# FFN weights of a transformer kernel turned by DMA transfers instead of TensorE, with POOL, ACT and DVE queues reordered

## The reference, cut to what matters

```python
def block_qdq_weight(w, block=32, bits=4):       # w_gate, w_up: (1376, 512), w_down: (512, 1376)
    wb = w.reshape(out_f, in_f // block, block)
    scale = jnp.maximum(jnp.max(jnp.abs(wb), axis=-1, keepdims=True) / 7, 1e-12)
    wq = jnp.clip(jnp.round(wb / scale), -8, 7) * scale
xq = act_qdq(x)                                  # 16 bits, one scale for the whole tensor
up = act_qdq(xq @ wu.T)
gate = act_qdq(xq @ wg.T)
sig = fixed_qdq(jax.nn.sigmoid(gate), 1 / 65536)
gate = act_qdq(gate * sig)
o = act_qdq(gate * up)
return o @ wd.T
```

## Time and profile before

| | |
|---|---|
| median of 3 runs | 828.37 us (827.33 to 829.54) |
| the profiled execution, time | 830.54 us |
| its span, first to last instruction | 828.5 us |
| TensorE busy | 728.5 us (88%) |
| DVE busy | 643.6 us (78%) |
| ACT busy | 513.9 us (62%) |
| POOL busy | 511.3 us (62%) |
| mean granted TensorE clock | 0.954 |

### The profile page before, as it was taken

One profiled execution on the slowest core, in us unless ns is written; L12 is line 12 of the kernel. 1 busy time (PEld: TensorE's weight loads), 2 busy tenths in 40 slices (PEclk: granted clock), 3 DMA queues, 4 the chain that ended last, 5 costly groups with the idle time before them and its releaser, 6 DMA issues.

```text
span 828.5 us, 13514 instructions
## 1 busy us (share of the span) xinstructions
PE 728.5 (88%) x3443; PEld 342.7 (41%) x3443; DVE 643.6 (78%) x1374; ACT 513.9 (62%) x968; POOL 511.3 (62%) x488
## 2 busy tenths in 40 slices
PE   0688999736695996999999999999999788999998
PEld 0234545313232452444444444444444253444443
DVE  6885667678799678888888888888888767656655
ACT  4656766556857436777777777777776643655540
POOL 1986675546566557778888888888884414344330
PEclk9999999976888898999999999999999999999998
DMA  7211232201225326788666666666655512332311
GB/s 320 89 65 39 65 101 67 62 26 51 39 51 95 121 70 133 178 191 180 124 146 144 144 144 145 142 146 144 152 102 102 102 39 80 107 110 84 114 38 51
DMA packets 164500, 89.08 MB, mean 108 GB/s; under 512 B 154081, under 2 KB 154337, under 8 KB 161522
## 3 DMA queue, kind: packets, MB, share of 16 engines
q1 hardware_dynamic: 164466, 88.67, 42.9%
HBM read 49.85 MB, written 1.05 MB: 61 GB/s over the span
## 4 chain that ended last, share of the span: by engine, by line
PE 60%; DVE 13%; POOL 12%; issue 9%; DMA 2%; ACT 2%; SPq 1%; DVEq 0%; POOLq 0%; ACTq 0%
PE ps L950 19%; PE ps L951 19%; PE ps L952 19%; POOL arena L464 4%; POOL arena L472 3%; DVE arena L1290 3%; DVE arena L1293 2%; PE ps L1138 1%; POOL arena L604 1%; DMA arena<-arena 1%; DVE arena L1287 1%; POOL arena L451 1%; ACT arena L647 1%; POOL arena L482 1%; DVE ss L1449 1%
## 5 line engine op out<-in xcount | busy, mean ns | idle before, releaser
L950 PE MATMUL ps<-arena 128*128 128x512 f16 (+2 forms) x996 | 385.9, 388 | 25.7 <-DVE arena L1293 11.8
L951 PE MATMUL ps<-arena 128*128 128x512 f16 (+2 forms) x996 | 384.6, 386 | 0.0
L952 PE MATMUL ps<-arena 128*128 128x512 f16 (+2 forms) x996 | 384.2, 386 | 0.0
L647 ACT ACTIVATE arena<-arena 128x512 f16<-128x512 f32 (+9 forms) x392 | 260.8, 692 | 98.1 <-POOL arena L604 29.6
L1293 DVE SCALAR_TENSOR_TENSOR arena<-ps,arena 128x512 f32<-128x512 f32 (+2 forms) x182 | 122.9, 702 | 53.4 <-ACT arena L647 45.9
L950 PEld LDWEIGHTS ps<-arena 128*128 128x128 f16 (+1 forms) x996 | 99.5, 100 | 148.2 <-issue 34.6
L952 PEld LDWEIGHTS ps<-arena 128*128 128x128 f16 (+1 forms) x996 | 99.5, 100 | 122.6 <-issue 11.3
L951 PEld LDWEIGHTS ps<-arena 128*128 128x128 f16 (+1 forms) x996 | 99.5, 100 | 111.7 <-issue 9.2
L604 POOL TENSOR_SCALAR arena<-arena,rden 128x512 f32<-128x512 f32 x128 | 114.9, 898 | 25.3 <-DVE rden L1639 16.1
L1287 DVE TENSOR_TENSOR arena<-arena 128x512 f16<-128x512 f32 (+2 forms) x146 | 108.7, 779 | 5.3 <-ACT arena L647 4.8
L846 ACT ACTIVATE arena<-arena,mneg 128x512 f32<-128x512 f32 x124 | 88.5, 715 | 36.8 <-DVE mneg L1619 36.8
(11 more groups left out here) (126 smaller groups left out, 702.4 us busy)
## 6 DMA issues: line engine op xcount, KB each, us to landing
arena<-in_moe_w SPq DMA_DIRECT2D x18, 768.0 KB, 4.4
arena<-in_ffn_w SPq DMA_DIRECT2D x33, 256.0 KB, 2.7
arena<-in_wq SPq DMA_DIRECT2D x8, 1024.0 KB, 5.3
arena<-in_wo SPq DMA_DIRECT2D x8, 1024.0 KB, 5.3
arena<-in_kv_w SPq DMA_DIRECT2D x4, 1024.0 KB, 5.1
arena<-arena SPq DMA_TRANSPOSE x144, 3.3
arena<-in_ctx SPq DMA_DIRECT2D x1, 2048.0 KB, 9.5
arena<-in_ctx_t SPq DMA_DIRECT2D x1, 2048.0 KB, 13.9
```

What stands on the lines that cost most here:

```text
L647: return a.activation(out_, in_, ACT.Copy, scale=scale, bias=bias)
L950: pe.matmul(out_, lhs[0], rhs[0], start=first, stop=False)
L951: pe.matmul(out_, lhs[0], rhs[1], start=False, stop=False)
L952: return pe.matmul(out_, lhs[1], rhs[0], start=False, stop=last)
```

## The change

- A chunk isn't transposed by TensorE. `scale_back` writes `deq[n % 4]` (DQ = 4 buffers), ACT's `weight_high` copies it (from SBUF) to the first half of `wt[n % 4]`, the low half goes to the second half, and SP turns both with one DMA transposition of 128 x 1024 f16 into `wfx[n % 11]` (`turn_w`). `tile` waits for the landing.
- The low halves of even chunks from 14 on are POOL's (`low`), the others DVE's.
- Scales and their inverses are made for two chunks at once (`pair_scales`); the factor SW = 64 goes into the scales and into the first rounding copy.
- Five raw buffers instead of four; the load of chunk n+6 stands behind the turn of chunk n in SP's list. `turn_k` stands behind all turns of chunks and behind a wait for their landing.
- Turn n of each list now holds: ACT `weight_high(n+2)`, `round_weights(n+3)`, `tile_out(n)`; POOL `low(n+2)` (its chunks), `scale_back(n+3)`, `divide(n+4)`; DVE maxima of n+6, low half of n+2 (its chunks), the extrema of tile n-2, on odd n the scales of a pair.
- Value units 8 to 15 use banks 2 and 3 in turn instead of bank 4 alone, and wait for the copy before the last one.
- The split of the key weights moves to gate tiles 15 to 20. `s16` has four buffers: sigmoid i waits for `gated(i-4)` instead of `gated(i-2)`. `k_pow` and `k_low` stand one turn earlier in POOL's list.

```diff
-RAW = 4
+RAW = 5
+DQ = 4
+SB = 4
...
+def low_owner(n):
+    return 0 if n >= FT + 2 and n % 2 == 0 else 1
+def low_count(n):
+    return sum(low_owner(m) == low_owner(n) for m in range(n + 1))
...
-        wf = [carve(104, (WS, D), F16), carve(115, (WS, D), F16)]
+        wfx = carve(104, (WS, 2 * D), F16)
+        wf = [wfx[:, :, 0:D], wfx[:, :, D:2 * D]]
+        wt = carve(56, (DQ, 2 * D), F16)
+        deq = carve(64, (DQ, D))
...
-        s16 = carve(10, (2, TOK), U16)
+        s16 = carve(8, (SB, TOK), U16)
...
-        deq = [carve(202, (D,)), carve(8, (D,))]
...
+        w_lo = [sem("w_lo0"), sem("w_lo1")]
+        w_tr = [sem(f"w_tr{i}") for i in range(DQ)]
...
+            def turn_w(n):
+                sp.wait_ge(w_lo[low_owner(n)], low_count(n))
+                if n >= WS:
+                    sp.wait_ge(f_ps, n - WS + 1)
+                sp.dma_start_transpose(wfx[:, n % WS].rearrange("p (a b) -> p a b", b=P),
+                                       wt[:, n % DQ]).then_inc(w_tr[n % DQ], 16)
...
+            ring(RAW)
...
-            plain_loop(sp, RAW, FT + 5, ring)
-            kw_load(3)
-            plain_loop(sp, FT + 5, NCH, ring)
+            for n in range(2):
+                turn_w(n)
+                ring(n + RAW + 1)
+            for n in range(2, NCH):
+                turn_w(n)
+                if n + RAW + 1 < NCH:
+                    ring(n + RAW + 1)
+                if n == FT + 1:
+                    kw_load(3)
+            for i in range(DQ):
+                sp.wait_ge(w_tr[i], 16 * ((NCH - 1 - i) // DQ + 1))
...
             def divide(n):
-                g.wait_ge(w_inv, n + 1)
+                g.wait_ge(w_inv, n // 2 + 1)
...
-                if n >= 2:
-                    g.wait_ge(w_t, n - 1)
-                g.tensor_tensor(deq[n % 2].rearrange("p (a b) -> p a b", b=QB), v, s, ALU.mult).then_inc(w_deq, 1)
+                if n >= DQ:
+                    g.wait_ge(w_lo[low_owner(n - DQ)], low_count(n - DQ))
+                g.tensor_tensor(deq[:, n % DQ].rearrange("p (a b) -> p a b", b=QB), v, s, ALU.mult).then_inc(w_deq, 1)
+            def low(n):
+                g.wait_ge(w_hi, n + 1)
+                g.tensor_tensor(wt[:, n % DQ, D:2 * D], deq[:, n % DQ], wt[:, n % DQ, 0:D], ALU.subtract)\
+                    .then_inc(w_lo[0], 1)
...
             def weights(n):
-                scale_back(n)
-                if n + 2 < NCH:
-                    divide(n + 2)
+                if n + 2 < NCH and low_owner(n + 2) == 0:
+                    low(n + 2)
+                if n + 3 < NCH:
+                    scale_back(n + 3)
+                if n + 4 < NCH:
+                    divide(n + 4)
...
+            scale_back(0)
...
-            scale_back(0)
-            for u in range(4, MT - 1):
-                v_low(u)
-            g.wait_ge(xt_ps, KD)
...
+            v_low(4)
+            v_low(5)
+            v_low(6)
+            scale_back(2)
...
-            weights(2)
+            weights(0)
...
-                    weights(3 + k)
+                    weights(1 + k)
...
-                weights(2 * j + 4)
+                weights(2 * j + 2)
...
-                weights(2 * j + 5)
+                if j < 4:
+                    weights(2 * j + 3)
...
-                weights(2 * j + 14)
-                weights(2 * j + 15)
+                weights(2 * j + 11)
+                if j == 2:
+                    kw_scale(3, 0)
+                    kw_scale(3, 1)
+                weights(2 * j + 12)
+                if j == 2:
+                    kw_scale(3, 2)
+                    kw_scale(3, 3)
...
-                if k < 3:
-                    weights(20 + k)
-                kw_scale(3, k)
-            weights(2 * FT + 1)
-            weights(2 * FT + 2)
-            for k in range(KD):
+                weights(17 + k)
...
-            for i in range(2, FT - 1):
-                weights(2 * FT + 1 + i)
-                u = i // 2 - 2
-                if i % 2 == 0 and u >= 0:
+            weights(2 * FT - 1)
+            weights(2 * FT)
+            for i in range(1, FT - 1):
+                weights(2 * FT + i)
+                u = i // 2 - 1
+                if i % 2 and u >= 0:
...
-            for u in range(3, 2 * MT):
+            for u in range(4, 2 * MT):
...
-                copy(w, w, 1.0, MAGIC).then_inc(w_mag, 1)
+                copy(w, w, SW, MAGIC).then_inc(w_mag, 1)
...
-                src = bank(2 + u % 2 if u < MT else 4)
+                src = bank(2 + u % 2)
...
+            def weight_high(n):
+                a.wait_ge(w_deq, n + 1)
+                if n >= DQ:
+                    a.wait_ge(w_tr[n % DQ], 16 * (n // DQ))
+                copy(wt[:, n % DQ, 0:D], deq[:, n % DQ]).then_inc(w_hi, 1)
...
-            for u in range(3, MT - 1):
-                v_out(u)
+            v_out(3)
+            v_out(4)
+            weight_high(0)
+            v_out(5)
+            v_out(6)
...
+            weight_high(1)
...
-            def weight_high(n):
-                a.wait_ge(w_t, n + 1)
-                if n >= WS:
-                    a.wait_ge(f_ps, n - WS + 1)
-                copy(wf[0][:, n % WS], bank(2 + n % 2), SW).then_inc(w_hi, 1)
...
             def tile_turn(n, dst):
-                weight_high(n + 1)
+                weight_high(n + 2)
...
-            weight_high(0)
...
-                if n >= 2 * FT - KD:
-                    kw_high(3, [n - 2 * FT + KD])
+                if FT + 6 <= n < FT + 6 + KD:
+                    kw_high(3, [n - FT - 6])
...
-                if i >= 2:
-                    a.wait_ge(gs_done, i - 1)
+                if i >= SB:
+                    a.wait_ge(gs_done, i - SB + 1)
...
-                if i < FT - 1:
-                    weight_high(2 * FT + i + 1)
+                if i < FT - 2:
+                    weight_high(2 * FT + i + 2)
...
-                if u >= MT:
-                    pe.wait_ge(v_cp, u)
-                elif u >= 2:
+                if u >= 2:
...
-                kv_product(c, m, bank(2 + u % 2 if u < MT else 4)).then_inc(v_ps, 1)
+                kv_product(c, m, bank(2 + u % 2)).then_inc(v_ps, 1)
...
-            pe.wait_ge(xt_lo, 1)
...
-            def weight_transposes(n):
-                pe.wait_ge(w_deq, n + 1)
-                if n >= 2:
-                    pe.wait_ge(w_lo, n - 1)
-                for k in range(4):
-                    mm = pe.transpose(bank(2 + n % 2)[:, k * P:(k + 1) * P], deq[n % 2][:, k * P:(k + 1) * P],
-                                      ident[:, :])
-                mm.then_inc(w_t, 1)
...
-                pe.wait_ge(w_lo, n + 1)
+                pe.wait_ge(w_tr[n % DQ], 16 * (n // DQ + 1))
...
-            def step(base, i, odd):
-                weight_transposes(base + i + 1)
-                tile(base, i, odd)
...
-            pe.wait_ge(v_cp, MT)
-            weight_transposes(0)
...
-                step(0, i, i % 2)
+                tile(0, i, i % 2)
...
-                    step(0, i, i % 2)
+                    tile(0, i, i % 2)
...
-                step(FT, i, (FT + i) % 2)
+                tile(FT, i, (FT + i) % 2)
...
-            weight_transposes(2 * FT + 1)
...
-            for u in range(5):
-                weight_transposes(2 * FT + 2 + 2 * u)
+            for u in range(6):
...
-                if u < 4:
-                    weight_transposes(2 * FT + 3 + 2 * u)
-            k_unit(5)
...
-            pe.wait_ge(w_lo, NCH)
+            for i in range(DQ):
+                pe.wait_ge(w_tr[i], 16 * ((NCH - 1 - i) // DQ + 1))
...
-            def scales(n, maxima):
-                own.wait(maxima)
-                s = one(dsc, n % SC)
-                return own.mark(ts(s, s, 1.0 / 7.0, ALU.mult, TINY, ALU.max))
-            def inverse_scales(n, scaled):
-                own.wait(scaled)
-                v.reciprocal(one(dsi, n % SC), one(dsc, n % SC)).then_inc(w_inv, 1)
-            def block_scales(n):
-                inverse_scales(n, scales(n, block_maxima(n)))
+            def pair_scales(n):
+                own.wait(own.n)
+                at = (n - n % 2) % SC
+                both = [flat(w[:, at:at + n % 2 + 1]) if n % 2 else w[:, at] for w in (dsc, dsi)]
+                own.link(ts(both[0], both[0], SW / 7.0, ALU.mult, SW * TINY, ALU.max))
+                v.reciprocal(both[1], both[0]).then_inc(w_inv, 1)
...
-                stt(one(wf[1], n % WS), bank(2 + n % 2), SW, one(wf[0], n % WS), ALU.mult, ALU.subtract).then_inc(w_lo, 1)
+                tt(wt[:, n % DQ, D:2 * D], deq[:, n % DQ], wt[:, n % DQ, 0:D], ALU.subtract).then_inc(w_lo[1], 1)
...
-            for n in range(3):
-                block_scales(n)
+            for n in range(4):
+                block_maxima(n)
+                if n % 2:
+                    pair_scales(n)
...
-                m = block_maxima(n + 3)
-                weight_low(n)
-                m = scales(n + 3, m)
+                if n + 6 < NCH:
```

(60 more changed lines are left out.)

6 lines of the change are left out of this document (3 added, 3 removed).

## The result

The changed kernel takes 826.65 us (median, 824.89 to 828.05), the kernel before 828.24 us (825.86 to 833.61), both on one chip. The ratio is 0.9971, 95% interval 0.9958 to 0.9985: faster by 2.4 us (1.6 us between the two medians), where 10.8 us were forecast. The direction was right, the size was not: 826.65 lies just above the range of 809 to 826, and the gain is one that the forecast itself called hard to tell from none (under 0.3%). The profiled execution has 825.1 us of span against 828.5, with a mean granted clock of 0.943 (0.954 before).

The account below looks back on a forecast made before the run. TensorE bounds up and early gate tiles; a row of work across engines bounds the last gate tiles and sigmoid stage; DVE times-up. -10.5 (to gate's end) - 0.3 (sigmoid) = -10.8: 819.7 profiled, 817.5 us median; own range 813 to 822, wide range 809 to 826.

Parts of the forecast that it names:

- Parameters of up keep their 2.7 us hole: End of up stage: hole unchanged, last value unit ends 110.7, first gate tile 113.5 against 118.4, -4.9 us.
- its last ends +35: Gate tail: DVE's last extrema end 35 us after tile 14, at 161.4 against 171.97; -10.5 us in all.
- not on the path: Pairs of scales: one multiply and reciprocal per two weights save at most 0.5 us of DVE a weight, off the path.
- A set: Transposition set on TensorE: 0.45 us each; 22 of 33 count where TensorE is the bound, 9.9 us at most.
- Pairs: Two tiles with one value unit: new latency hides, so a pair takes 7.75 us instead of 8.64.
- the POOL-ACT loop: Rounding, scale-back and divide take 3.5 us per weight; hidden in pairs, the bound where tiles follow without value units.
- the key turn takes it back: Sigmoid stage: ACT waits for turn_k(0) behind all weight landings, losing the 5.5 us gained; 48.5 us, -0.3 us.
- Rival 1: Sigmoid stage: key turn isn't late, landing before ACT's copy; -10.5 - 6.5, 811 us; chance 0.12.
- rivals 2 and 4: 2: POOL-ACT loop shows, pairs 8.2, 823 us, chance 0.24. 4: no split fits, pairs 9.4, 828 us, chance 0.08.
- Rival 3: Transposition landing too long: gain gone at 5.9 us, at 6.5 us the run takes 834 us; chance 0.08.
- the old price of a late gate tile: Last gate tiles, kernel before: one takes 5.9 us, TensorE waiting for POOL's scale-back, then DVE's low half.
- The low half was priced 0.7: DVE's low half of a weight: 0.7 us, rounded up from four in 2.48.

Follow-up runs that it names:

- the 16 matmuls: Changed kernel plus 16 TensorE matmuls, whose results nothing reads, in the hole ahead of the parameters of up: 825.56 us, ratio 0.9947 to the kernel before.
- the four combined kernels: Changed kernel with key turns earlier and five up conversions later (821.56 us); adding low halves on DVE (822.80), 16 matmuls (821.09), maxima 16 behind up's parameters (820.20).

## Why the prediction was wrong

**The step that failed first** is "Parameters of up keep their 2.7 us hole, since tile_out(10) ends level with the last value unit". The value unit ended 0.7 us later than forecast (111.4 against 110.7), and ACT was no obstacle (tile 10 out at 110.6). But DVE had its own turn 10 and a pair of scales ahead of three extrema groups, and its queue set the moment: first gate tile at 116.12 instead of 113.5. I had walked ACT, POOL and TensorE through this place, and DVE not; in the queue order its extra work could be read. The longer hole then cost the clock level, which the forecast allowed for only ahead of tile 20: 4.7 us for a tile of 2.6. Together the second gate tile came 4.7 us later than forecast: 0.7 from the value unit, 1.9 from the longer hole, 2.1 from the clock. The earlier parameters with DVE's turn moved show the part of the hole, the 16 matmuls that of the clock.

**The second term mis-sized** is the gate tail, "its last ends +35". The walk of POOL's queue was right: from the end of tile 14 (131.4) tile 20 started at +22.5 as forecast, tile 21 went out from +31.0 as forecast, and the lower clock in tile 20, which the forecast had allowed for, was hidden ahead of it. DVE's last work ended at +37.1: extrema and conversions as counted, but a pair of scales stood between, which the forecast had called "not on the path" and which took 1.3 us there, and a conversion took 1.19 us instead of 0.54. So the parameters of gate came at 168.52 and not 161.4: 4.7 up to the second gate tile, 2.1 from the tail and 0.3 between them, -3.5 us where -10.5 stood. That DVE's list sets this end is shown by the five conversions moved away; what the stretching alone costs, no run shows.

**What held.** A set is worth 0.44 us where TensorE is the bound. Pairs take 7.77 us (7.75 forecast), the POOL-ACT loop 3.46 (3.5), the turn lands 3.1 us after its issue (4.9 at most), from the end of low half 20 (150.7) to tile 20 it is 3.1 us where 3.5 were taken with 0.3 for semaphores, tile 0 starts at 69.74 (70.0). In the sigmoid stage the forecast was that sigmoids and loop gain 5.5 and the key turn takes it back, 48.5 us: it took 48.43, 42.98 without the key turn's place in the queue, and 53.14 without the two further buffers. Rival 1's 6.5 us were measured as 5.4. Times-up was unchanged. The times of rivals 2 and 4 (823 and 828) bracket the result, but the mechanism of neither was there: the loop did not show in the pairs. Rival 3 needed landings over 5.9 us; none came, even with a second turn for each weight. The 5.9 us that the forecast read as the old price of a late gate tile is one gap of several: from set to set the kernel before has 3.2, 5.9 and 6.5 us from 151.87 on. The sum does not use it.

**What the sum missed besides.** The low half was priced 0.7 by a row that reads PSUM. The new one reads two operands from SBUF. Groups by shape, DVE, changed kernel, 70 to 222.4 us:

```profile
L1313 DVE TENSOR_TENSOR arena<-arena 128x512 f16<-128x512 f32 x21 | 17.9, 851 | 19.6 <-ACT arena L692 19.4
```

In the kernel before, the 15 of this form that read PSUM average 684 ns. Of the 21 the 16 that start while a POOL instruction runs average 0.90 us and take up to 1.28; the other five take 0.68 to 0.69. The mean excess of 0.17 us a weight doesn't explain the result, but it falls ahead of both sets of parameters.

The 4.1 us that the profile leads by at the end of times-up (258.3 against 262.4) are 3.4 at its end and 2.4 by the runs; where the rest goes was not followed, and is about what single executions differ by. Nor is it settled why the four combined kernels lie 1 to 2 us apart by their runs in another order than in their profiles.

## What to carry to other kernels

Taking work off the busiest engine buys only the stretch up to the next point where everything is gathered; there the question is which engine's list ends last, so every engine must be walked through it, the one that looks half idle too. A transfer queue is an in-order list like any other: a short, urgent transfer placed behind the last of a long row of others, and behind a wait for their landing, cost 5.4 us here, what twelve transposition sets of 0.44 us cost. And an edit that gains alone because it fills another's wait has to be tried again once that wait is gone.

## What the runs showed of the hardware

A DVE instruction with both inputs in SBUF was held by POOL: a subtraction of 128x512 fp32 takes 0.69 us alone and up to 1.63 us beside POOL (in the kernel with all low halves on DVE), while one-input reductions stay at 0.67. One-input scalings are not spared: in the changed kernel a conversion of 128x512 takes 0.54 us or less with POOL idle and up to 1.46 beside it, the multiply of a pair of scales 0.17 to 0.18 and up to 1.13; the 1.19 and 1.02 us in the gate tail both start inside a POOL instruction, and the kernel before has such rows too (up to 1.36 and 1.04). The row of 1.32 us above, started 0.38 us into a POOL subtraction of 1.16, ends about as if it had begun where POOL's ended. The Trainium skill (SBUF — State Buffer, "Who interferes with whom") says that a DVE instruction with two SBUF inputs contends with a GpSimd instruction that reads SBUF; the rows agree.

TensorE's clock fell to its lower level after a hole of some 4.7 us holding only three tiny matmuls, and did not in the kernel with 3.6 us of matmuls in it. It fell as well after the 3.74 us of idle time before tile 20 and after the hole of 3.3 us in the kernel with DVE's turn 10 moved. With a second turn for each weight, a wait of 2.89 us before tile 0 was followed by the lower level (matmuls 0.42 us apart from the fifth on), where 2.36 us in the changed kernel was not.

Transpositions of 128 x 1024 f16 landed in 3.2 us even while the DMA share of the stage was 1.00.
